# Scaled keys and chunk inverse through DRAM into one tile, with a new order of the work

## The reference, cut to what matters

```python
# x: (8, 2048, 256), 16 heads of d = 16, lam and beta scalars
x_act = tanh(x)
static_out = x_act @ W.T
q = k = heads(x_act); v = heads(static_out)
# per head and batch, over the 2048 tokens:
#   S = lam*S;  u = beta*(v_t - S^T k_t);  S += k_t u^T;  o_t = S^T q_t
y = static_out + merge(o)
a = layernorm(y) * gamma + lnbeta
x1 = layernorm(x + a)
h = silu(x1 @ wg.T) * (x1 @ wu.T)      # wg, wu, wd: int32 weights / 127, hidden 768
out = layernorm(x1 + h @ wd.T)
```

## Time and profile before

| | us |
|---|---|
| median of 3 runs | 1876.73 |
| lowest, highest | 1870.12, 1882.23 |
| the profiled execution | 1866.64 |
| its span, first to last instruction | 1864.9 |
| mean granted TensorE clock, share of full | 0.824 |
| busy: PE, DVE, ACT, POOL | 1401.9, 1424.7, 1100.3, 782.9 |

### The profile page before, as it was taken

The page is one execution under the profiler, slowest core; times in us unless marked ns, Lnnn a source line. Parts: engine busy times, 40 slices in busy tenths (PEclk is TensorE's granted clock), DMA queues, the critical chain, the costliest instruction groups (busy, mean ns, idle before and its releaser), DMA issues.

```text
span 1864.9 us, 53894 instructions
## 1 busy us (share of the span) xinstructions
PE 1401.9 (75%) x21032; PEld 1080.7 (58%) x21032; DVE 1424.7 (76%) x3479; ACT 1100.3 (59%) x2339; POOL 782.9 (42%) x1106
## 2 busy tenths in 40 slices
PE   1344877788888878888888777788877888888764
PEld 0244656566666656666666566666655666666542
DVE  8257878788888878887888887788778887788741
ACT  0223666567666666666666666666666666666544
POOL 6012444344444444454444444444344444454442
PEclk9855887789888878888888788888887888888877
DMA  2445544445555455545644554454455544544200
GB/s 71 87 92 111 99 107 113 106 110 114 112 108 114 113 108 118 105 113 107 113 107 111 109 114 104 107 113 101 110 108 118 105 115 113 110 106 110 68 26 23
DMA packets 704383, 191.01 MB, mean 102 GB/s; under 512 B 624000, under 2 KB 691584, under 8 KB 704128
## 3 DMA queue, kind: packets, MB, share of 16 engines
q1 hardware_dynamic: 704128, 187.57, 47.3%
HBM read 103.55 MB, written 67.11 MB: 92 GB/s over the span
## 4 chain that ended last, share of the span: by engine, by line
SPq 39%; DMA 18%; PE 16%; DVE 10%; issue 8%; ACT 7%; POOL 1%; ACTq 0%; POOLq 0%; DVEq 0%
SPq L977 11%; DMA scr_t<-t 7%; SPq L986 6%; SPq L962 5%; PE pc L175 5%; SPq L947 4%; SPq L938 4%; DMA y_out<-v 4%; DMA xa<-L_attn_x 3%; PE pf L232 3%; SPq L920 3%; SPq L992 2%; DMA scr_x<-xt 2%; PE pd L272 2%; PE pg L240 2%
## 5 line engine op out<-in xcount | busy, mean ns | idle before, releaser
L879 POOL TENSOR_TENSOR hlo<-gate,hhi 128x512 f16<-128x512 f32 x192 | 228.9, 1195 | 325.1 <-ACT hhi L710 324.9
L175 PE MATMUL pc<-R,tb 128*128 128x32 f16 x4096 | 158.1, 189 | 161.7 <-DVE R L362 141.7
L175 PEld LDWEIGHTS pc<-R,tb 128*128 128x128 f16 x4096 | 147.1, 118 | 181.7 <-DVE R L362 156.5
L175 PE MATMUL pc<-S,e 128*128 128x32 f16 x4096 | 157.6, 188 | 61.8 <-DVE S L383 61.7
L175 PEld LDWEIGHTS pc<-U,kb 128*128 128x128 f16 x4096 | 152.0, 118 | 81.4 <-DVE U L370 79.1
L175 PEld LDWEIGHTS pc<-S,e 128*128 128x128 f16 x4096 | 153.1, 118 | 77.4 <-DVE S L383 67.6
L175 PE MATMUL pc<-U,kb 128*128 128x32 f16 x4096 | 159.4, 190 | 49.7 <-DVE U L370 49.6
L209 PEld LDWEIGHTS pf<-xb,e 128*128 128x128 f16 x4096 | 152.8, 118 | 60.1 <-DMA e<-scr_x 42.1
L272 PE MATMUL pd<-wd_t,hhi 128*128 128x256 f16 x768 | 176.7, 276 | 13.7 <-DVE xr L481 8.2
L209 PE MATMUL pf<-xb,e 128*128 128x32 f16 x4096 | 156.3, 191 | 37.4 <-DMA e<-scr_x 36.1
L272 PE MATMUL pd<-wd_t,hlo 128*128 128x256 f16 x768 | 176.3, 276 | 0.0
(11 more groups left out here) (118 smaller groups left out, 3297.4 us busy)
## 6 DMA issues: line engine op xcount, KB each, us to landing
xa<-L_attn_x SPq DMA_DIRECT2D x128, 128.0 KB
scr_x<-xt SPq DMA_DIRECT2D x64, 256.0 KB, 2.1
xb<-scr_x SPq DMA_DIRECT2D x256, 64.0 KB, 2.8
e<-scr_x SPq DMA_DIRECT2D x256, 64.0 KB, 3.6
scr_g<-gs SPq DMA_DIRECT2D x32, 512.0 KB, 2.9
gh<-scr_g SPq DMA_DIRECT2D x256, 64.0 KB, 2.2
kb<-k SPq DMA_DIRECT2D x512, 32.0 KB, 2.3
scr_t<-t SPq DMA_DIRECT2D x64, 256.0 KB
```

Source lines behind the costliest of these rows:

```text
L175: last = pe.matmul(pc2[:, :, cols], stationary(h, a), moving[:, :, cols], start=a == 0, stop=a == 1)
L879: pool.tensor_tensor(hlo[:, t, :], gate[:, t % 2, :], hhi[:, t, :], ALU.subtract).then_inc(SEM["hl"], 1)
```

## The change

The scaled keys no longer go from SBUF to SBUF. They are stored to DRAM in one transfer of 256 KB per half (`sp_store_scaled`), next to the inverse, in one DRAM tensor scr_tk with the order half, kind, head, batch, row. kb and tb become the two parts of one tile tk, and one set of 8 transfers of 64 KB per half (`sp_load_blocks`) fills both. It waits for both stores. TensorE waits once per half, for tk, ahead of the product with the inverse. The gram is stored with the token outermost in DRAM and read back in one transfer of 512 KB. ScalarE may overwrite k16 once its store to DRAM has landed.

The order of the work is new on every engine. The last inverse columns, the first half's split, three of the six feed-forward tiles' gates and two ups, three of the multiplies and the scaling of the keys move from the start of a step to the end of the one before. On ScalarE, `act_static_out(0)` moves from behind `act_update(2)` to ahead of `act_rest(2)`; on TensorE, `pe_transpose_keys(0)` moves ahead of `pe_inverse_by_rest(2)`; on SP, x is loaded ahead of the second inverse store, and the store of y is the last transfer of a step.

```diff
-        tb = sb("tb", [P, 2, H, B, C, 2, 2], F16)
-        kb = sb("kb", [P, 2, H, B, DH, 2, 2], F16)
+        tk = sb("tk", [P, 2, 2, H, B, C, 2, 2], F16)
+        tb, kb = tk[:, :, 0], tk[:, :, 1]
-        scr_g = nc.dram_tensor("scr_g", [B, C, H, T], F32).ap()
-        scr_t = nc.dram_tensor("scr_t", [B, 2, H, C, T], F16).ap()
+        scr_g = nc.dram_tensor("scr_g", [C, B, H, T], F32).ap()
+        scr_tk = nc.dram_tensor("scr_tk", [2, 2, H, B, C, T], F16).ap()
...
         def pe_keys_by_update(pe, q, p, w):
             pe.wait_ge(SEM["u"], n_of("u", q, w + 1))
-            if w % 2 == 0:
-                pe.wait_ge(SEM[f"kb{w // 2}"], n_of(f"kb{w // 2}", q))
...
         def sp_store_gram(sp, q, p):
-            sp.dma_start(scr_g.rearrange("b i h t -> (b i) (h t)"),
+            sp.dma_start(scr_g.rearrange("i b h t -> b i (h t)"),
                          gs[:, :, :, :].rearrange("p h j n -> p (h j n)")).then_inc(SEM["gd"], 16)
         def sp_load_gram(sp, q, p):
-            for b in range(B):
-                sp.dma_start(gh[H * b:H * (b + 1), :, :, :].rearrange("h i j n -> h i (j n)"),
-                             scr_g[b].rearrange("i h t -> h i t")).then_inc(SEM["gh"], 16)
+            sp.dma_start(gh[:, :, :, :].rearrange("p i j n -> p i (j n)"),
+                         scr_g.rearrange("i b h t -> (b h) i t")).then_inc(SEM["gh"], 16)
         def sp_store_inverse(sp, q, p, g):
-            sp.dma_start(scr_t[:, g].rearrange("b h j t -> b h (j t)"),
+            sp.dma_start(scr_tk[g, 0].rearrange("h b j t -> b h (j t)"),
                          t16[:, g].rearrange("p j i z m -> p (j i z m)")).then_inc(SEM[f"td{g}"], 16)
+        def sp_store_scaled(sp, q, p, g):
+            sp.wait_ge(SEM["k16"], n_of("k16", q, g + 1))
+            sp.sem_inc(s_hop, 1)
+            sp.wait_ge(SEM[f"tk{g}"], n_of(f"tk{g}", q - 1))
+            sp.dma_start(scr_tk[g, 1].rearrange("h b i t -> (b i) h t"),
+                         k16[:, g].rearrange("p h k z m -> p h (k z m)")).then_inc(SEM[f"kd{g}"], 16)
+        def sp_load_blocks(sp, q, p, g):
+            sp.wait_ge(SEM[f"kd{g}"], n_of(f"kd{g}", q))
+            sp.sem_inc(s_hop, 1)
+            sp.wait_ge(SEM["sp"], n_of("sp", q - 1, 2 * g + 2))
+            sp.sem_inc(s_hop, 1)
+            sp.wait_ge(SEM[f"td{g}"], n_of(f"td{g}", q))
+            for b in range(B):
+                sp.dma_start(tk[C * b:C * (b + 1), g, :, :, b].rearrange("j a h i z m -> j (a h) (i z m)"),
+                             scr_tk[g, :, :, b].rearrange("a h j t -> j (a h) t")).then_inc(SEM[f"tk{g}"], 16)
```

More of the change, by code:

```diff
@@ L278, in pe_step @@
             if live(s - 2):
[L279 to L286, removed]
                 pe_up(pe, s - 2, p, 2)
+                pe_up(pe, s - 2, p, 3)
                 pe_gate(pe, s - 2, p, 3)
@@ L290, in pe_step @@
                 pe_gram(pe, s + 1, 1 - p, 0, range(0, 8))
+            if live(s - 2):
+                pe_gate(pe, s - 2, p, 4)
+            if live(s):
+                pe_keys_by_state(pe, s, p, 0)
+            if live(s + 1):
                 pe_gram(pe, s + 1, 1 - p, 0, range(8, 16))
@@ L310, in pe_step @@
             if live(s + 1):
+                pe_gram(pe, s + 1, 1 - p, 3, range(0, 8))
                 pe_gram(pe, s + 1, 1 - p, 3, range(8, 16))
@@ L331, in pe_step @@
                 pe_keys_by_state(pe, s, p, 2)
-                pe_inverse_by_rest(pe, s, p, 2)
             if live(s + 1):
                 pe_static_out(pe, s + 1, 1 - p, 3)
+            if live(s + 2):
+                pe_transpose_keys(pe, s + 2, p, 0)
+            if live(s):
+                pe_inverse_by_rest(pe, s, p, 2)
+            if live(s + 2):
+                pe_transpose_keys(pe, s + 2, p, 1)
             if live(s):
                 pe_keys_by_update(pe, s, p, 2)
[L337 to L342, removed]
             if live(s - 1):
@@ L345, in pe_step @@
                 pe_transpose_x1(pe, s - 1, 1 - p, 1)
+            if live(s):
+                pe_keys_by_state(pe, s, p, 3)
+            if live(s - 1):
+                pe_up(pe, s - 1, 1 - p, 0)
+                pe_gate(pe, s - 1, 1 - p, 0)
+            if live(s):
+                pe_inverse_by_rest(pe, s, p, 3)
+            if live(s - 1):
+                pe_gate(pe, s - 1, 1 - p, 1)
+                pe_gate(pe, s - 1, 1 - p, 2)
+                pe_up(pe, s - 1, 1 - p, 1)
             if live(s):
@@ L484, in dve_step @@
         def dve_step(dve, s, p):
[L485 to L492, removed]
             if live(s - 1):
                 dve_statistics(dve, s - 1, 1 - p, 3)
+                dve_moments(dve, s - 1, 1 - p)
             if live(s):
[L496 to L506, removed]
+                dve_rest(dve, s, p, 0)
             if live(s - 2):
@@ L579, in dve_step @@
             if live(s):
-                dve_state(dve, s, p, 3)
+                dve_rest(dve, s, p, 3)
             if live(s + 1):
                 dve_invert(dve, s + 1, 1 - p, range(11, 13))
+            if live(s + 2):
+                dve_scale_keys(dve, s + 2, p, 0)
+            if live(s + 1):
+                dve_invert(dve, s + 1, 1 - p, range(13, 15))
+            if live(s - 1):
+                dve_multiply(dve, s - 1, 1 - p, 0)
+            if live(s):
+                dve_update(dve, s, p, 3)
+            if live(s + 1):
+                dve_store_inverse(dve, s + 1, 1 - p, 0)
+            if live(s - 1):
+                dve_multiply(dve, s - 1, 1 - p, 1)
+            if live(s):
+                dve_state(dve, s, p, 3)
+                dve_statistics(dve, s, p, 2)
+            if live(s + 2):
+                dve_scale_keys(dve, s + 2, p, 1)
+            if live(s - 1):
+                dve_multiply(dve, s - 1, 1 - p, 2)
         def act_rest(act, q, p, w):
```

215 lines of the change are left out of this document (100 added, 115 removed).

## The result

The changed kernel takes 1967.32 us (1965.89 to 1972.49), the kernel before 1877.32 in the same rounds: ratio 1.0488, interval 1.0448 to 1.0527. It is slower by 5%, where 2.5% faster was forecast. The profiled execution's span grew from 1864.9 to 1964.1, at the same mean granted TensorE clock (0.821, before 0.824), so the clock is not the cause.

What follows compares the result with a forecast made beforehand. Two close limits: SP's issue time and the loop through the output's store. Gram to static output 18.3 plus compute 33.3 made 51.6 us a step against 53.07; −46 over 31 steps, plus 10.1 for the median: 1831 us, range 1765 to 1893.

Steps and rivals of the forecast that it cites:

- SP's issues: Issue time of SP's transfers: some 340 us less in all, 11 us a step, worth about 0.9 a step in itself.
- the first inverse: Its store, landing and combined loads at the step's end: 11.1 to 12.5 us against 11.7 of other VectorE work; costed nothing.
- Stretch B: From the finished gram through SP and DMA to ScalarE's copy of the static output: 18.3 us, before 20.0.
- dear end: The high end of the stretch from gram to static output, with slow landings and loads: 20.2 to 21.5 us.
- The gram's way back: Gram's single 512 KB load: lands 10 to 11 us after the gram; VectorE's 1.5 wait covered by the static output's.
- Stretch A: Compute from ScalarE's copy of the static output to the next finished gram: 33.3 us, before 32.7.
- The rule that spoke against the change: Gram store, 8 batches outermost, uses 8 engines, not 16: lands 2 to 3 us later, costing the sum 0 to 1.
- Late output: Rival, chance 0.18: static output ahead of act_rest(2) waits for y landing at 20.2 to 21.5; slower, 1911 us.

Runs made afterwards that it cites:

- e2: The kernel before with only the gram's way back changed (new layout, one store, one load): 1829.5 us, ratio 0.9747.
- e5: The changed kernel with the old order of work on every engine and the gram's way as before; scaled keys and inverse still through DRAM into tk: 1932.1 us, 1.0308.
- e1: The changed kernel with the gram's way as before (old layout, one store, eight loads), all else changed: 1870.3 us, ratio 0.997.
- e7: The changed kernel with the inverse's partitions head, batch; gram stored with 128 rows outermost, loaded once; inverse halves stored as 128 rows: 1843.0 us, 0.983.
- e8: The changed kernel with the static output's copies moved back behind act_update(2) and the key transposes behind window 2's inverse product and update: 1963.3 us, 1.0475.
- e12: The kernel before with head-major partitions (e11) and the four residual loads moved on SP behind the two inverse stores: 1794.0 us, 0.9616.
- e10: The changed kernel with both head-major partitions (e7) and x loaded ahead of the gram's store (e9): 1824.6 us, 0.9749.
- e4: The changed kernel with the four loads of x moved on SP from behind the gram's store to behind the gram's load: 2007.1 us, 1.0692.
- e6: The old order of work with all the change's transfers: e5 plus the gram's new layout and single load: 1912.9 us, 1.0206.
- e9: The changed kernel with the four loads of x moved on SP from behind the gram's store to ahead of it: 1888.5 us, 1.0087.
- e11: The kernel before, order, kb and tb untouched, with head-major partitions for the gram and inverse and one gram load, as in e7: 1798.5 us, 0.9611.

## Why the prediction was wrong

*SP's issues:* right. Combined loads 0.486, the scaled stores 0.388 and the gram load 0.379 (I took 0.6), SP's part in the chain 7%. What I drew from it held only in part: fewer issues are a gain where nothing else is lost (e2), but the one tile costs 3.1% in the old order (e5), where the product with the inverse waits for the keys as well. I had costed the first inverse at nothing, late by up to 1. In the new order that is so (13.9 us of waiting in all); there the new order pays for it.

*Stretch B:* this step failed, and the term in it is the gram's store. I had 18.3 from the gram to the static output, the trace has 22.7 (22.5 in the median step). Term by term: x takes 5.40 of SP instead of 2.65, which puts the inverse store at 6.3 instead of 3.4; it lands after 6.5 instead of 5.1; the loads 4.3 for 4.2; the last y 3.4 for 3.5. Nearly all of it comes from the slow forms of store: with only the gram's way as before (e1) the stretch is 19.3, with head-major partitions (e7) 18.5, and there the period, 52.25, is close to the 51.6 of my sum. Of the gram's store I wrote that it "costs the sum nothing but what it shifts behind it, 0 to 1", with 2.9 and 5.5 as its bounds. It takes 7.6 with an inverse store beside it and 8.8 with x. The bound of 5.5 came from a store of 256 KB; this one carries 512, so the row was of the wrong size as well. And what it shifts is 4.4, not 0 to 1: x and the inverse store queue behind it, and the loads of tk and the stores of y follow them on SP. My dear end had a slip of addition besides: 8.9 + 6.4 + 2.1 + 4.99 is 22.4, not 21.5; and SP's issuing in the old stretch, 15.3 by my count, adds up to 15.0 (0.80 + 4.18 + 4.75 + 2.64 + 2.66).

*The gram's way back:* this failed with it, from the same store. I had the load landing at 10 to 11 and a covered wait of 1.5. It landed 15.2 after the gram, and VectorE waits 5.3 in that step. Nor is the wait covered by the one for L635: e8 takes that one away and is as slow.

*Stretch A:* right. 33.3 forecast, 34.6 in the step shown, 33.6 left after the static output by the medians. The sum's form was right too: 22.5 + 33.3 = 55.8, measured 56.12. But the price that I put on the new order there, 0.6 more than 32.7, isn't seen: 32.7 was one step, and by the medians the kernel before has 33.7. The step shown runs over the transposed keys and the landing of e; the chain of the whole run does so in 5 of 27 steps.

*The rule that spoke against the change:* it named the term that decided, and I priced it too low. The store of the gram with 128 rows outermost lands after 2.8 to 2.9 (e7, e12), and after 5.1 behind four loads of x (e10); with the 8 batches outermost it lands after 6.8 (e2, median of the steps in which SP waits for it) to 8.8; the inverse store of the same 256 KB after 2.0 with 128 rows and nothing of that form ahead (e12), after 4.1 with 8 batches. The Trainium skill, "DMA: Bandwidth & Descriptors", section "Why a DMA increments its semaphore by 16 and not by 1", has such a transfer on 8 engines instead of 16. The sign agrees. Half the engines would at most double the landing (an estimate from that page's 8 and 16), and the growth here, 2.9 to between 6.8 and 7.8, is more than that. The profile doesn't show which engines a transfer used, so the mechanism is argued, not shown.

*Late output*, the rival with 0.18, had the sign and the turning point (a landing at 19.8; it was 22.6), but not the size: 1911, measured 1967. That it had the sign was luck in part: its cause (y itself landing after 5) and its place (ahead of `act_rest(2)`) were both wrong.

## What to carry to other kernels

Before a store is reshaped, look which dimension comes out outermost on each side, and take its price from a transfer of the same form and the same size. Price a slow transfer together with everything queued behind it: here moving four loads from behind it to ahead of it gave back four fifths of the loss. Look for a second road before calling a wait covered: here the late gram reached the next step both through SP's queue and through VectorE's mask, and neither a sooner mask (e4, where x came later) nor the end of the wait for y (e8) gained anything by itself. And the same transfer has another price in another order: the reshaped gram gains 2.5% where eight loads of 32 KB fill its landing (e2), 1 point where they carry 64 KB (e6 against e5), and costs 5.2 points where x and a store stand between it and its load.

## What the runs showed that I had not expected

Issuing behind a slow transfer takes SP longer: the four loads of x behind the gram's store take 5.40 us to issue (5.0 in the median step), 2.64 to 2.67 with nothing slow ahead (e9) and 3.2 behind the gram's load (e2, e4). A store of 128 rows lands late behind loads of x or of the residual, whose DRAM side begins with the 8 batches: that of the inverse after 4.4 behind the residual and 2.0 ahead of it (e11, e12), that of the gram after 5.1 behind x and 2.8 ahead of it (e10, e7). Whether the form of those loads or only their bytes do it isn't separated. And a partition order (head, batch instead of batch, head), together with the single gram load and without a change to any compute instruction, is worth 3.9% in the kernel before and 6.6 points in the changed one.
